# Half of five batches' softmax transposes, moved from TensorE to VectorE blocks and DMAs (gated cross-attention and ternary FFN)

## The reference

```python
xn = layernorm(x, axis=-1)
theta = einsum('ld,bdt->btl', theta_w, ctx) + theta_b        # l = 128, t = 512
phi   = einsum('ld,bdt->blt', phi_w, xn) + phi_b[:, None]
p     = softmax(einsum('btl,bls->bts', theta, phi), axis=-1) # 512 x 512 for each batch
g     = einsum('ld,bdt->btl', g_w, xn) + g_b
tx    = einsum('bts,bsl->blt', p, g)                         # needs p with s on the partitions
h     = relu((tx - mean) * rsqrt(var + 1e-5) * gamma + beta) # mean, var over all of (l, t)
x     = x + tanh(g_xattn) * (out_w @ h + out_b + ctx)
# FFN: layernorm, rmsnorm, int8 activations, ternary w1, w2, w3:
x     = x + tanh(g_ffn) * bitlinear(silu(bitlinear(n, w1)) * bitlinear(n, w2), w3)
```

## Time and profile before

| | |
|---|---|
| median of 3 runs | 300.6 us (300.51 to 300.93) |
| profiled execution, its own time | 300.9 us |
| its span in the profile | 298.9 us |
| granted TensorE clock | 1.0 of full speed |
| PE, DVE, ACT, POOL busy | 294.7, 241.2, 197.2, 193.8 us |
| attention: first theta of batch 1 to the end of step 7 | 14.05 to 118.95 us |

### The profile page before, as it was taken

How to read it: one execution, slowest core, us unless ns; L and a number is a source line. 1 busy time by engine, 2 the same in 40 slices (tenths; PEclk the granted TensorE clock), 3 DMA queues, 4 the chain that set the end, 5 groups by cost and what they waited for, 6 DMA issues and landing times.

```text
span 298.9 us, 4419 instructions
## 1 busy us (share of the span) xinstructions
PE 294.7 (99%) x1350; PEld 160.1 (54%) x1350; DVE 241.2 (81%) x541; ACT 197.2 (66%) x347; POOL 193.8 (65%) x293
## 2 busy tenths in 40 slices
PE   8999999999999999999999999999999999999996
PEld 5765757575757566644444444444444444444444
DVE  3799889796969797899888788887986896876872
ACT  1389898989989877699954736455465547445720
POOL 3351789594949286666988778586786786665610
PEclk9999999999999999999999999999999999999999
DMA  7999970094320002010326366144324342561456
GB/s 252 411 418 414 405 281 3 16 385 163 140 71 0 0 3 35 0 38 0 70 52 77 83 127 114 40 110 106 72 70 106 73 111 64 102 109 50 93 101 183
DMA packets 52936, 37.00 MB, mean 124 GB/s; under 512 B 43056, under 2 KB 43696, under 8 KB 51888
## 3 DMA queue, kind: packets, MB, share of 16 engines
q1 hardware_dynamic: 52624, 36.45, 42.5%
q10 hardware_dynamic: 288, 0.27, 0.3%
HBM read 22.02 MB, written 4.19 MB: 88 GB/s over the span
## 4 chain that ended last, share of the span: by engine, by line
PE 93%; ACT 4%; DMA 2%; SPq 0%; DVE 0%; issue 0%
PE bank L1149 37%; PE bank L1167 17%; PE bank L1093 9%; PE bank L1071 7%; PE bank L1108 5%; PE bank L1086 4%; PE bank L1058 4%; PE bank L1048 4%; PE bank L1037 4%; ACT wq L492 2%; DMA c_sb<-ctx_in_dram 2%; PE bank L1180 1%; ACT prob L539 1%; ACT probT L535 1%; PE bank L1120 0%; PE bank L1116 0%
## 5 line engine op out<-in xcount | busy, mean ns | idle before, releaser
L1149 PE MATMUL bank<-wq,stage 128*128 128x512 bf16 x512 | 113.3, 379 | 0.0
L1149 PEld LDWEIGHTS bank<-wq,stage 128*128 128x128 bf16 x512 | 50.1, 98 | 61.5 <-issue 2.3
L816 DVE SCALAR_TENSOR_TENSOR stage<-bank,s,stage 128x512 f32<-128x512 f32 x64 | 47.5, 744 | 22.2 <-PE bank L1149 18.2
L573 ACT ACTIVATE xn<-stage 128x1024 f32<-128x1024 f32 x31 | 32.8, 1057 | 46.2 <-DVE stage L816 46.2
L565 ACT ACTIVATE stage<-bank,s 128x512 f32<-128x512 f32 x64 | 43.2, 681 | 16.3 <-PE bank L1149 14.3
L1167 PE MATMUL bank<-wq,prob 128*128 128x512 bf16 x224 | 50.5, 379 | 0.0
L428 POOL TENSOR_SCALAR stage<-stage,hsc 128x1024 f32<-128x1024 f32 x30 | 33.4, 1123 | 20.3 <-DVE hsc L847 20.3
L346 POOL TENSOR_SCALAR prob<-prob,rsum 128x512 f32<-128x512 f32 x29 | 19.6, 694 | 30.9 <-DVE rsum L718 30.9
L821 DVE TENSOR_REDUCE m<-stage 128x1 f32<-128x1024 f32 x31 | 37.7, 1216 | 0.8
L1167 PEld LDWEIGHTS bank<-wq,prob 128*128 128x128 bf16 x224 | 21.9, 98 | 26.4
L1071 PE MATMUL bank<-ph,th 128*128 128x512 f32 x96 | 36.0, 487 | 0.0
(11 more groups left out here) (117 smaller groups left out, 434.3 us busy)
## 6 DMA issues: line engine op xcount, KB each, us to landing
stage<-w1t_dram SPq DMA_DIRECT2D x4, 1024.0 KB, 11.5
stage<-w2t_dram SPq DMA_DIRECT2D x4, 1024.0 KB, 14.6
stage<-w3t_dram SPq DMA_DIRECT2D x4, 1024.0 KB, 5.8
x<-x_dram SPq DMA_DIRECT2D x7, 512.0 KB, 10.8
c_sb<-ctx_in_dram SPq DMA_DIRECT2D x7, 512.0 KB, 6.3
out_dram<-stage SPq DMA_DIRECT2D x14, 256.0 KB, 2.3
pc<-pack_c_dram SPq DMA_DIRECT2D x1, 640.0 KB, 15.5
x<-x_dram SPq DMA_DIRECT2D x2, 256.0 KB, 3.4
```

The lines of the kernel that those rows point to most:

```text
L573: A.activation(junk, h_sb[t % 2][:, half * HF:(half + 1) * HF], ACT.Square, accum_out=ssq[:, half:half + 1]).then_inc(sq_done, 1)
L816: V.scalar_tensor_tensor(h_sb[k][:, c * 512:(c + 1) * 512], up_banks(n)[1][:, :], s12[:, u % 2, 1, k:k + 1], sil[n % 3], ALU.mult, ALU.mul ...
L1149: last = mm(bank[:, :], turned[:, row:row + P], wq[:, at:at + 512], start=q == 0, stop=q == KI - 1)
```

## The change: what it does

For batches 1 to 5 (`by_blocks`) the second half of the key columns (chunks c = 2 and 3) is no longer turned by PE. DVE turns all 32 x 32 blocks of that half with two STREAM_TRANSPOSE instructions into the new tile `blocks` (`turn_blocks`), and SP moves the blocks into their partitions with 16 DMAs of 32 rows x 1 KB for each batch (`move_blocks`, 32 KB each, 80 DMAs in all). `values(i, 2)` and `values(i, 3)` read the result, `placed`, one step later: after phi of step i + 2. So that a DMA row is contiguous, the tokens of these batches are taken in another order: ACT and DVE write theta with a step of 128 elements (`in_rows`), and `p_copy` writes with a step of 4.

Round it: `x_norm` of batches 2 to 7 goes from DVE to POOL; for batches 1 to 5 POOL scales two chunks and ACT the other two; ACT's weight pieces are taken two at a time (128 x 2048) in three slots per step; on DVE `tx_mean` comes later in the step, and in step 7 the first FFN tiles' `prep_max` and `prep_scale` stand before `tx_dev`; `scores(i, 2)` uses bank 4 where it used bank 0. The diff, cut:

```diff
+        blocks = sb("blocks", [P, TC * 2 * P])
+        placed = sb("placed", [P, 4, 2 * P])
...
+        def by_blocks(i):
+
+            return 1 <= i <= B - 3
...
+            def move_blocks(i):
+
+                sp.wait_ge(blocks_ready, 2 * i)
+                sp.wait_ge(tx_done, i)
+                for q in range(4):
+                    for k in range(4):
+                        sp.dma_start(placed[32 * k:32 * (k + 1), q], blocks[32 * q:32 * (q + 1), 2 * k * P:2 * (k + 1) * P])\
+                            .then_inc(blocks_moved, 16)
...
             load_x(4)
+            move_blocks(1)
             load_x(5)
             load_c(4)
+            move_blocks(2)
             load_x(6)
             load_x(7)
             load_weight(2, 0)
             load_c(5)
+            move_blocks(3)
             load_weight(2, 1)
             load_weight(2, 2)
             load_c(6)
+            move_blocks(4)
             load_weight(2, 3)
             load_c(7)
+            move_blocks(5)
...
+            def x_norm(b):
+                pool.wait_ge(xrstd_ready, b + 2)
+                pool.wait_ge(proj_done, 3 * b)
...
-                for c in range(chunks):
+                for c in range(2 if by_blocks(i) else chunks):
...
-                2: ((M, 0, 6), (M, 0, 7), None, (M, 1, 0), (M, 1, 1), (M, 1, 2), (M, 1, 3)),
+                1: ((M, 0, 3, 1), None, (M, 0, 4)),
+                2: ((M, 0, 6), None, (M, 1, 0)),
...
+                if i == 1 or by_blocks(i - 1):
+                    normalise(i - 1)
...
+            def turn_blocks(i, k):
+
+                if k == 0:
+                    dve.wait_ge(pnorm_ready, 4 * i + 4)
+                    if i >= 2:
+                        dve.wait_ge(blocks_moved, 256 * (i - 1))
+                V.transpose(blocks[:, :].rearrange("p (s k r c) -> p k c s r", s=4, k=2, c=TC)[:, k],
+                            prob[:, i % 2, :, (2 + k) * P:(3 + k) * P].rearrange("p c (s r) -> p c s r", r=32))\
+                    .then_inc(blocks_ready, 1)
...
             def values(i, c):
-                pe.wait_ge(pT_ready, 4 * i + c + 1)
+                if by_blocks(i) and c >= 2:
+                    pe.wait_ge(blocks_moved, 256 * i)
+                else:
+                    pe.wait_ge(pT_ready, turn_no(i, c) + 1)
```

More of the change, by code:

```diff
@@ L706, in low_part @@
                 dve.wait_ge(high_ready, i + 1)
-                V.scalar_tensor_tensor(dst[:, 1], bank[:, :], biases[:, column:column + 1], dst[:, 0],
-                                       ALU.add, ALU.subtract).then_inc(low_ready, 1)
+                high, low = (in_rows(i, dst[:, part]) if dst is th else dst[:, part] for part in range(2))
+                V.scalar_tensor_tensor(low, bank[:, :], biases[:, column:column + 1], high, ALU.add, ALU.subtract)\
+                    .then_inc(low_ready, 1)
             def row_max(i, c):
@@ new lines, in third_step @@
+            def third_step():
+                dve.wait_ge(gates_ready, 1)
+                dve.wait_ge(pc_loaded, 16)
+                sum_inverse(1)
+                tx_mean(0)
+                x_stats(3, 0)
+                low_part(2, th, b_th, 0, th_ready, thl_ready)
+                turn_blocks(1, 0)
+                turn_blocks(1, 1)
+                low_part(2, ph, b_ph, 1, ph_ready, phl_ready)
+                x_stats(3, 1)
+                tx_dev(0)
+                tx_gamma(0)
+                weight_part(0)
+                row_max(2, 0)
+                tx_var(0)
+                residual(2)
+                row_max(2, 1)
+                weight_scale(0)
+                tx_norm(0)
+                row_max(2, 2)
+                row_max(2, 3)
@@ L880, in _ @@
-                if i + 1 < B:
-                    x_stats(i + 1, 1)
-                else:
-                    prep_scale(0)
-                if i >= 3:
-                    tx_dev(i - 2)
-                if i >= 1:
-                    low_part(i, ph, b_ph, 1, ph_ready, phl_ready)
-                if i == 2:
-                    tx_dev(0)
-                if i == 1:
-                    weight_abs(0)
-                if i >= 3:
-                    add_out(i - 3, 1)
-                if i >= 2:
-                    tx_gamma(i - 2)
@@ L905, in _ @@
                     prep_mean(1)
[L906 to L923 removed]
+                if by_blocks(i - 1):
+                    turn_blocks(i - 1, 0)
+                    turn_blocks(i - 1, 1)
+                low_part(i, ph, b_ph, 1, ph_ready, phl_ready)
+                if weight is not None:
+                    weight_scale(weight)
+                tx_mean(i - 2)
+                add_out(i - 3, 0)
+                if i == 7:
+                    prep_max(0, 0)
+                    prep_max(0, 1)
+                    prep_scale(0)
+                tx_dev(i - 2)
+                tx_gamma(i - 2)
+                add_out(i - 3, 1)
+                row_max(i, 0)
+                tx_var(i - 2)
+                residual(i)
+                row_max(i, 1)
+                tx_norm(i - 2)
                 row_max(i, 2)
[L925 to L926 removed]
                 row_max(i, 3)
[L928 to L931 removed]
+                if i in (3, 6):
+                    weight_part({3: 1, 6: 2}[i])
+            for o in range(DH):
+                x_stats(0, o)
+            x_norm(0)
+            for i in range(B):
+                if i < 2:
+                    first_steps(i)
+                elif i == 2:
+                    third_step()
+                else:
+                    later_step(i)
             sum_inverse(B - 1)
```

256 lines of the change are left out of this document (133 added, 123 removed).

## The result

The changed kernel took 307.07 us (median of 4 runs, 306.47 to 307.28) beside 300.73 us for the kernel before (median of 4): a ratio of 1.0208, 95% interval 1.019 to 1.0225. The forecast of 297.2, with its range of 295.7 to 300.5, was wrong by sign.

A forecast was written before the change was run, and what follows sets the result against it. PE was taken to bound steps 3 to 7 at full clock. Gains of 4.4 and 0.3 less losses of 0.45, 0.4 and 0.5 gave 3.35 us, from 300.6 to 297.2 us; range for all 295.7 to 300.5.

The forecast's parts named there:

- The failed step: POOL in the attention steps: two `x_norm` replace two scalings, work stays under 12.5 us, `x_norm` ends near 14.
- The sum: Whole kernel: 4.4 + 0.3 gained, 0.45, 0.4 and 0.5 lost, giving 3.35 us less.
- The strided writes: Rival, ACT and DVE writes: a second pass costs 2.8 us in all, time 300.0; chance 0.17 in part or whole.
- SP's issues: 16 per batch at 0.42 us, hidden; as rival, above 0.60 PE waits, 308.3 at 0.74; chance 0.17 with worse DVE chain.
- The 4.4 us of PE: PE, steps 2 to 6: ten `turn_p` of 0.44 us go; steps 3 to 6 shrink from about 15.4 to 14.5.
- The 0.69 us of a transpose: DVE: each of two STREAM_TRANSPOSE per batch priced at 0.69 us, like the reduction of 128x512; 1.2 from above.
- The loss at ACT's double piece in step 1: ACT, step 1: two weight pieces ahead of the last `p_copy` delay `values(0, 3)`; 0.45 us lost.
- The wait for gamma in step 7: DVE, step 7: `prep_max` twice and `prep_scale` ahead of `tx_dev` make gamma late for `values(6, 0)`; 0.4 us lost.

The follow-up runs named there:

- e4: The changed kernel with all strided writes made contiguous, leaving the rearrangement of rows out: 303.87 us, ratio 1.0092.
- e1: The changed kernel with POOL's `x_norm` adding a negated mean in place of subtracting the mean: 303.56 us, ratio 1.0076.
- e5: The changed kernel with e1's addition and a correct layout without strided writes, PE reading placed blocks in pieces of 32 columns: 301.45 us, ratio 1.0023.
- e7_half: e5 with only 8 of 16 block rows moved in batches 2 to 5, half of the rearrangement left out: 299.77 us, ratio 0.9962.
- e6: e5 with the 16 moves per batch replaced by one store to HBM and four loads back: 303.68 us, ratio 1.0091.
- e16_rounds: e13 with two of POOL's four first rounding pieces put behind the scaling, one step later: 298.99 us, ratio 0.9939.
- e9: e5 with, in step 2, ACT scaling before theta's high part and DVE turning blocks before theta's low part: 299.82 us, ratio 0.9959.
- e13: e9 with batch 3's moves ahead of all w3 loads on SP, and ACT taking w3's pieces one slot later: 299.36 us, ratio 0.9952.
- e8: e5 with the four loads of w3 issued by ACT and no longer by SP: 304.12 us, ratio 1.0113.
- e17: e13 with 4 of each batch's 16 moves issued by ACT: 307.58 us, ratio 1.0231.
- e10: e5 with the edits of e8 and e9, step 7's `tx_dev` and gamma before `prep_scale`, step 1's double ACT piece cut: 304.87 us, ratio 1.0140.

## Why the prediction was wrong, step by step

**The failed step** is "POOL trades two scalings for two `x_norm` and stays under 12.5", with "`x_norm` on POOL ends near 14, wanted by phi at 16". POOL was 15.4 us busy in step 3 and 13.3 in steps 4 and 5; in step 4 the pair started at 14.0 and ended at 18.2 into the step. I took the price, 0.7 us, from the scalings beside it, which multiply; with the subtraction it is 2.1 us, with an addition 1.0. The sum has no term for POOL at all. I bounded the transposes from both sides but not this, although no row showed POOL doing this operation. I also left out what it queues behind (`tx_root`, which waits for `tx_var` and so for PE's `var_mm`) and what queues behind it: the roundings, the scaling, DVE's transposes, `tx_mean` and the moves. Adding a negated mean in its place gives 4.0 us back.

**The strided writes** were a rival with a chance of 0.17. It came true beside the late `x_norm`, and its prices (0.53 on DVE, 0.44 on ACT) had the right size: 0.45 measured for a block transpose, and on ACT 0.55 for `p_copy` and 0.47 for theta. That a second pass is the reason is not shown. Its total was not: I had 2.8 us from work sums, and the runs give 3.5 and 3.6, 3.5 of them in e4 while POOL was still late. My argument against it, "a write of one element per cycle may not care where it goes", had no row behind it. The Trainium skill, SBUF — State Buffer, Door 1, states a penalty for accesses that change their 16-byte line each time, and here the trace agrees: 1.14 against 0.69 us.

**SP's issues** cost 0.65, not 0.42; the bounds named 0.60 as the limit and 0.64 as the end of the gain. The step that failed is taking the interval from two large loads, when no row had a transfer of this kind. By the rival's own sum 0.65 would make PE wait 0.8 us per batch, 4.0 in all. The wait was small in the changed kernel only because POOL was later still. It stood out as 3.3 us in e1 and 2.9 in e5, in three batches each. The Trainium skill, DMA: Bandwidth & Descriptors, rules for kernel authors, speaks against many small transfers; e7_half agrees in the sign, 1.8 us for 8 of 16, though what binds there is rather SP's time to issue them (10.4 us, against 1.9 for one to land); e6, with 5 larger transfers by way of HBM, lost 2.0 us.

**What was right.** The 4.4 us of PE: with waits gone, steps are 14.4 to 14.6 us in e7_half (14.4 to 14.9 in e16_rounds), and step 2 is 11.22 there (11.2 forecast). The 0.69 us of a transpose, once its writes are contiguous. The loss at ACT's double piece in step 1: 0.4 us, seen when it was cut. The wait for gamma in step 7: 0.55, forecast 0.4.

**The sum.** By e16 the attention part is 102.57 us against 104.90, 2.3 us of the 3.35 forecast; the part behind takes 180.3 us instead of 179.95. The missing 1.0 us of the attention part lies in steps 1, 6 and 7 by 0.3 to 0.4 each (14.4, 14.9 and 18.0 us). What releases PE there was not tried apart and stays open. In ratios, e5 gives back 5.6 us of the 9.9 between forecast and measurement, the orders of e9, e13 and e16 another 2.5, and about 1.7 is left.

## What to carry to other kernels

An operation that moves to another engine needs its price on that engine with that operator and those operands, and its start from the queue there, which is set by the latest wait ahead of it. When three covered costs grow at once, repair them in the order in which they bind: each repair shows the next wait, and one alone returns only part. A bulk load issued beside a short transfer that the bottleneck engine waits for can make it late (5.05 us to land instead of 1.9 in e8), also from another engine's queue, so issue it behind.

## What the runs showed of the hardware

- `tensor_scalar` on 128x512 f32 takes POOL 2.1 us with `subtract, mult` and 1.04 with `add, mult` and the mean in another tile (medians 2.08 and 0.84); DVE takes 0.54 with `subtract, mult` (median). POOL's `add, mult` of `c_sb` with two pointers takes 0.76.
- ACT and DVE writes whose neighbours lie 16 or 512 bytes apart take 1.13 to 1.15 us instead of 0.59 to 0.74. A matmul that reads its moving data in pieces of 32 f32 takes 592 ns like a contiguous one.
- A DMA of 32 KB from SBUF to SBUF costs 0.59 us of SP's queue (median) and 0.63 to 0.68 from start to start. It lands in 1.9 us (median), but took 5.05 us beside loads of 1 MB in e8.
- Four such issues hold ACT for 2.4 us (e17).
- In e8, after 2.3 us of idle, PE was granted 0.50 of its clock for some 2 us. Likewise e6, e10 and e17, with waits of 2.2 to 2.5 us, have a mean clock of 0.993 or 0.994 over the span; e5 and e7, with waits up to 1.8 us, have 1.000.
